# Two linear attentions: transposes in another bank, VectorE's work reordered, GpSimd's rotated sum split

## The chip, the cores and the metric

The kernel runs on one core of a Trainium2 chip. The metric is the device time of one execution in microseconds; the kernel before has a median of 1056.55 us over three runs. All data is float32.

## The reference

`x` has 16 batches of 512 tokens of 128 features. Two blocks follow one another, each an attention and a feed-forward part, both around layer norms, shifts and scales that depend on the batch. The change touches the two attentions alone:

```python
def _linear_attention(q, k, v):
    def step(carry, qkv_t):
        S, z = carry
        qt, kt, vt = qkv_t
        S = S + kt[..., :, None] * vt[..., None, :]
        z = z + kt
        num = jnp.einsum('bhi,bhij->bhj', qt, S)
        den = jnp.sum(qt * z, axis=-1, keepdims=True)
        return ((S, z), num / (den + EPS))
...
q = jax.nn.elu(to_tbhd(q)) + 1.0
k = jax.nn.elu(to_tbhd(k)) + 1.0
...
q = _rotate(q, cos, sin)
k = _rotate(k, cos, sin)
retention = jnp.einsum('bhsd,bhtd->bhst', q, k) * SCALING
retention = retention * decay[None]
out = jnp.einsum('bhst,bhtd->bhsd', retention, v)
out = (out - mean) * jax.lax.rsqrt(var + EPS)
gate = jax.nn.silu(x @ Wg.T)
return gate * out @ Wo.T
```

The first is a causal linear attention with 16 heads of 8 features and the feature map elu + 1. The second is a causal retention with rotated queries and keys, a group norm per head and a gate. `_rotate(x)` is x times a cosine plus the half-swapped x times a sine: two products and a sum.

## The kernel before

A function `attention` (line 291) writes both, with `layer` 0 and 1. A batch is four tiles of 128 tokens, a pair is two tiles, and a step works on one pair `(b, u)`, with tiles `ta = 2u` and `tb = 2u + 1`. I call u = 0 step A and u = 1 step B. Each engine has its own program in order (`pe_step`, `act_step`, `vec_step`, `pool_step`, lines 672 to 790); the engines meet by semaphores alone. A loop runs over the middle batches, and the first and last ones are written out.

For one tile: TensorE projects q, k and v of the next batch's tile into the bank pQ (`pe_qkv`, 410). ScalarE copies v out (`act_qkv`, 419). In the first attention it makes exp and relu of q and k there, and VectorE joins them to the feature map (`vec_qk`, 446). In the second VectorE makes three products with cosines and sines into `ra` and `rb` (452, 456, 457), and GpSimd adds them for q and k of both tiles of a pair (`pool_rope`, 465). pQ is one bank: the next projection waits until it has been read (`qk_free`).

GpSimd then makes all outer products of k and v for a pair (`pool_kv`, 475). TensorE sums them along tokens with a triangular matrix, three matrix products per tile, which I call the states (`pe_states`, 485), into the banks pS. VectorE multiplies each by q (`vec_product`, 574), GpSimd adds the halves of the result (`pool_halve`, 591) and VectorE reduces them (`vec_sum`, 602).

What earlier tiles contribute goes through a running state: `pe_state_sum` (500) adds the tile's key times value in pR, VectorE masks it (`vec_state`, 583), and `pe_inter` (493) multiplies it with the transposed queries into the bank pI, from where ScalarE copies it (`act_inter`, 538). The queries are transposed by `pe_transpose_q` (512) into the fourth quarter of pQ and copied out as qT by `act_qT` (546). Since TensorE must not write into a bank that is being read, this transpose waits until the next batch's tile has left pQ (`v_ready`, `qk_free`).

Two steps later the normalised y is transposed in pairs into pI (`pe_transpose_y`, 521) and copied out (`act_yT`, 553 or 556); in the second attention GpSimd multiplies it by the gate at the end of its step (`pool_gate`, 564). Three steps later it is projected (`pe_project`, 530) and added to x (`vec_residual`, 653). The gate is a silu over a whole batch, once per batch at the end of ScalarE's step A, between two loads of its function tables (`act_gate`, 665 and 666); step B begins behind it.

The order of one step of VectorE is: products 0, 1 and 2 of tile ta, with the feature map or rotation of the pair ahead's second tile behind the first or second of them, then reductions, mask, products of tile tb, and behind its second product the feature map or rotation of the next batch's tile ta.

## Time and profile before

| what | us |
|---|---|
| median of three runs (1055.17 to 1057.34) | 1056.55 |
| profiled execution | 1054.64 |
| its span | 1052.8 |
| PE busy | 860.5 (82%) |
| DVE busy | 829.7 (79%) |
| POOL busy | 711.0 (68%) |
| ACT busy | 609.6 (58%) |

PE is TensorE, DVE VectorE, ACT ScalarE, POOL GpSimd, PEld TensorE's weight loads. Products of the first attention's tiles run from 53.6 us on, and the last of the second attention's start at 675.5; between the two lies the first feed-forward part. "Idle before" in brackets is how long the engine stood still in front of an instruction, and behind the arrow what ended it. Instructions of one engine may overlap by some hundredths of a microsecond, so the distance of two starts is the better price of a step. An "x6" merges instructions of one line, and some matrix products are missing from the trace.

### The profile page before, as it was taken

Reading aid. Unit: us, or ns where it says so; the run is one execution under the profiler, and the core shown is the slowest. Engines: PE = TensorE matmul, PEld = TensorE weight load, DVE = VectorE, ACT = ScalarE, POOL = GpSimd, SP = SyncE. Lnnn points to the kernel's source line nnn. Section 1 sums busy time; section 2 is a strip of 40 time slices with the busy share of each in tenths; the row PEclk is TensorE's granted clock in tenths of the full one; section 3 lists DMA queues with packets and bytes.
Section 4 is the critical chain, followed back from the end, with each engine's and each line's share of the span. In section 5 each row is a group of like instructions: output and inputs, shape, how many; then the busy total and the mean of one; then the engine's idle time right before and its main releaser. Section 6 shows DMA issues by size and latency. Waiting matters only on the chain. (4 is left out here: it accounts for less than half of the span.)

```text
span 1052.8 us, 24355 instructions
## 1 busy us (share of the span) xinstructions
PE 860.5 (82%) x5240; PEld 622.6 (59%) x5240; DVE 829.7 (79%) x2581; ACT 609.6 (58%) x1524; POOL 711.0 (68%) x450
## 2 busy tenths in 40 slices
PE   5699999999968977888898988639888731999993
PEld 5456666666645754555555655426656521999993
DVE  5468888888875994888888888767988770899995
ACT  2545555555427965565656566347765212999992
POOL 4478878878853535999999999645599562255554
PEclk9799999999987998999999999859999855999997
DMA  8520000000000000000000000064566654544420
GB/s 243 165 66 2 0 0 0 0 0 0 0 1 5 0 1 1 11 11 20 10 20 10 20 10 20 21 184 109 149 207 208 192 193 143 159 131 134 133 68 20
DMA packets 64934, 70.11 MB, mean 67 GB/s; under 512 B 8965, under 2 KB 52178, under 8 KB 64740
## 3 DMA queue, kind: packets, MB, share of 16 engines
q1 hardware_dynamic: 50612, 47.20, 16.2%
q0 software_dynamic: 6368, 16.89, 4.7%
q10 hardware_dynamic: 7872, 5.08, 1.7%
q8 instruction: 33, 0.54, 0.2%
q14 instruction: 49, 0.40, 0.1%
HBM read 32.32 MB, written 24.50 MB: 54 GB/s over the span
## 5 line engine op out<-in xcount | busy, mean ns | idle before, releaser
L475 POOL TENSOR_TENSOR a_kv<-a_qk,a_vv 128x2304 f32<-128x2304 f32 (+1 forms) x64 | 252.0, 3938 | 37.1 <-DVE a_qk L446 32.6
L485 PE MATMUL a_pS<-a_kv,utri 128*128 128x360 f32 (+3 forms) x768 | 259.7, 475 | 10.7 <-POOL a_kv L475 10.7
L574 DVE TENSOR_TENSOR a_tt<-a_pS,a_qk 128x360 f32<-128x360 f32 (+3 forms) x384 | 201.5, 527 | 75.4 <-PE a_pS L485 75.2
L485 PEld LDWEIGHTS a_pS<-a_kv,utri 128*128 128x128 f32 x768 | 140.5, 191 | 96.2 <-issue 29.8
L591 POOL TENSOR_TENSOR a_tt<-a_tt 128x1152 f32<-128x1152 f32 (+1 forms) x64 | 144.7, 2260 | 37.7 <-DVE a_tt L574 37.6
L2016 POOL DMA_INDIRECT out_dram<-x_o,x_place x71 | 69.1, 974 | 76.1 <-DVE x_o L2003 75.1
L602 DVE TENSOR_REDUCE a_nd<-a_tt 128x144 f32<-128x720 f32 (+3 forms) x128 | 104.3, 817 | 1.0 <-POOL a_tt L591 0.9
L538 ACT ACTIVATE a_tt<-a_pI 128x144 f32<-128x144 f32 (+1 forms) x96 | 39.8, 415 | 96.0 <-PE a_pI L493 95.9
L1596 POOL DMA_INDIRECT ys<-m_S,m_dest x64 | 63.0, 984 | 35.2 <-issue 12.7
L546 ACT ACTIVATE a_qT<-a_pQ 128x128 f32<-128x128 f32 x96 | 26.5, 276 | 98.9 <-PE a_pQ L410 83.3
L1954 PE MATMUL x_pZ<-w,x_hT 128*128 x568 | 75.9, 277 | 1.4 <-issue 1.4
L1905 ACT ACTIVATE x_w<-w 128x644 f32 x71 | 52.4, 740 | 31.4 <-PEq L1737 26.3
L1954 PEld LDWEIGHTS x_pZ<-w,x_hT 128*128 128x128 f32 x568 | 69.0, 192 | 1.9 <-issue 1.7
L410 PE MATMUL a_pQ<-W,a_hT 128*128 128x384 f32 x122 | 55.2, 535 | 12.6 <-issue 7.2
L410 PE MATMUL a_pQ<-wqkv,a_hT 128*128 128x384 f32 x122 | 55.5, 537 | 8.5 <-issue 4.5
L380 ACT ACTIVATE a_xn<-X,nmr,rstd 128x128 f32 (+1 forms) x128 | 60.8, 484 | 1.8 <-DVE nmr L275 1.8
L287 DVE BATCH_NORM_STATS2 bn<-X 128x6 f32<-128x128 f32 (+1 forms) x256 | 55.9, 273 | 4.8 <-DMA X<-xs 4.7
L465 POOL TENSOR_TENSOR a_qk<-a_ra,a_rb 128x512 f32<-128x512 f32 x32 | 40.7, 1270 | 26.6 <-DVE a_rb L457 16.8
L530 PEld LDWEIGHTS a_pO<-wgate,a_yT 128*128 128x128 f32 x256 | 39.8, 199 | 26.3 <-issue 12.4
L530 PE MATMUL a_pO<-wgate,a_yT 128*128 (+1 forms) x256 | 41.4, 286 | 13.6 <-DVE a_y L644 11.7
L1936 ACT ACTIVATE x_hT<-x_pA,x_w 128x128 f32<-128x128 f32 x142 | 43.8, 360 | 8.4 <-PE x_pB L1928 8.2
L1945 DVE TENSOR_SCALAR x_hT<-x_pB,x_w 128x128 f32<-128x128 f32 x142 | 42.8, 343 | 6.8 <-PE x_pB L1928 6.8
(299 smaller groups left out, 2103.4 us busy)
## 6 DMA issues: line engine op xcount, KB each, us to landing
x_yl<-ys SPq DMA_DIRECT2D x71, 193.5 KB, 2.4
X<-xs SPq DMA_DIRECT2D x16, 256.0 KB, 5.3
kx<-m_kc SPq DMA_DIRECT2D x64, 64.0 KB
ax<-m_pc SPq DMA_DIRECT2D x64, 64.0 KB
m_S<-X SPq DMA_DIRECT2D x16, 256.0 KB, 3.6
xs<-X SPq DMA_DIRECT2D x15, 256.0 KB
w<-in_L_ffn_W_dram SPq DMA_DIRECT2D x1, 2048.0 KB
m_S<-gw ACTq DMA_DIRECT2D x6, 256.0 KB, 2.9
```

What stands on the lines that cost most here:

```text
L287: v.bn_stats(K.bn[:, ds(n, 1), :].rearrange("p a f -> p (a f)"), x[:, ds(n, 1), :].rearrange("p a f -> p (a f)"))\
L380: act.activation(xn[:, t, :], tile(K.X, 4 * b + t), ACT.Identity, bias=column(K.nmr, 4 * b + t), scale=column(K.rstd, 4 * b + t)).then_inc ...
L410: pe.matmul(bank_of(b, t, start)[:, 0:3 * P], hT[:, t * P:(t + 1) * P], wqkv, start=True, stop=True).then_inc(qkv_ps, 1)
L475: pool.tensor_tensor(kv[:, t:t + 2, :, :, :].rearrange("p t h j i -> p (t h) j i"), kk.unsqueeze(2).to_broadcast([P, 2 * H, J, D]), rows.u ...
L485: pe.matmul(pS[c][:, 0:(h1 - h0) * SC], K.utri[:, :], flat[:, h0 * SC:h1 * SC], start=True, stop=True).then_inc(u_done, 1)
L530: mm = pe.matmul(pO[:, k * P:(k + 1) * P], yT[:, k, :], tile(K.wgate[:, 0 if layer == 0 else 2, :, :], b), start=True, stop=True)
L574: v.tensor_tensor(tt[:, t, h0:h1, :, 0:D], pS[c][:, 0:(h1 - h0) * SC].rearrange("p (h j i) -> p h j i", i=D, j=J), q[:, h0:h1, :].unsqueez ...
L591: pool.tensor_tensor(two(D // 2), two(D // 2), two(0), ALU.add).then_inc(half_done, 1)
L602: v.tensor_reduce(nd[:, t % 2, :, :], tt[:, t, :, :, D // 2:rows], AX.X, ALU.add).then_inc(red_done, 1)
L1596: pool.indirect_dma_start(out=A["ys"], out_offset=bass.IndirectOffsetOnAxis(ap=dest[:, g // 2 % 2, at:at + 1], axis=0), in_=S[:, 4 * (g % ...
L1954: mm = pe.matmul(pZ[j % 2][:, 0:P], hT[:, j % 2, c * P:(c + 1) * P], K.w2[:, ds(e, 1), c, :].rearrange("p a f -> p (a f)"), start=(c == 0) ...
L2016: pool.indirect_dma_start(out=token_rows, out_offset=bass.IndirectOffsetOnAxis(ap=place[:, j:j + 1], axis=0), in_=o[:, j % 4, :], in_offse ...
```

## The change

1. The query transpose writes to pI, behind the inter-tile product, and no longer to pQ. It waits for pI's readers in place of pQ's. The projection loses its wait for `qT_ready`.
2. TensorE projects the next batch's tile directly behind the state sum. The output projection, the gate, the transposes of y and the query transpose follow. In the first attention the two tiles of y are transposed in the two halves of the step and copied out one by one; in the second both in the second half.
3. VectorE makes the feature map or rotation of the next batch's tile ta before the products of tile tb; the residual moves behind the mask.
4. In the second attention VectorE adds the rotated products of the queries (`vec_rope_q`), GpSimd those of the keys. A semaphore `q_ready` tells of the queries.
5. ScalarE copies v before qT, and takes the normalisation and the copies of y to the end of a half; the silu with its table loads stands behind both.
6. GpSimd multiplies by the gate one step later, at the step's beginning, before the keys' sum.

```diff
@@ waits of pe_qkv, vec_qk
-                wait(pe, qT_ready, 3 * b - 3 + t)
+                wait(v, q_ready, 2 * b + t // 2)
@@
+        def vec_rope_q(v, b, u):
+            t = 2 * u
+            v.wait_ge(rope_read, 4 * b + t + 2)
+            v.wait_ge(rope_b, 2 * (4 * b + t + 2))
+            wait(v, t_done, 3 * (4 * b + t - 2))
+            wait(v, q_T, 3 * b - 3 + t + 1)
+            v.tensor_tensor(qk[:, 0, t:t + 2, :], ra[:, :, 0:P], rb[:, :, 0:P], ALU.add).then_inc(q_ready, 1)
@@ pool_rope
-            slot_free(pool, b, t + 1)
-            four = lambda r: r[:, :, :].rearrange("p t (a f) -> p a t f", a=2)
-            pool.tensor_tensor(qk[:, :, t:t + 2, :], four(ra), four(rb), ALU.add).then_inc(qk_ready, 1)
+            wait(pool, kv_ready, 2 * b - 2 + u + 1)
+            wait(pool, p_done, 3 * b - 3 + min(t + 2, 3))
+            pool.tensor_tensor(qk[:, 1, t:t + 2, :], ra[:, :, P:2 * P], rb[:, :, P:2 * P], ALU.add).then_inc(qk_ready, 1)
@@ pe_transpose_q
-            pe.wait_ge(v_ready, m)
-            pe.wait_ge(qk_ready, qk_count(b, t))
-            pe.wait_ge(qk_free, m)
+            pe.wait_ge(q_ready, qk_count(b, t))
+            wait(pe, inter_ready, 3 * b + t - 1)
             wait(pe, qT_ready, 3 * b + t - 1)
-            pe.transpose(pQ[:, QT:QT + P], qk[:, 0, t, :], K.ident[:, :]).then_inc(q_T, 1)
+            wait(pe, yT_read, y_issued(b, t - 1))
+            pe.transpose(pI[:, QT:QT + P], qk[:, 0, t, :], K.ident[:, :]).then_inc(q_T, 1)
@@ pe_transpose_y
+            evacuated(pe, b, t)
+            if layer == 0:
+                pe.transpose(pI[:, YT:YT + P], y[:, t % 2, :], K.ident[:, :]).then_inc(y_T, 1)
+            else:
+                pe.transpose(pI[:, YT:YT + P], y[:, 0, :], K.ident[:, :])
+                pe.transpose(pI[:, YT + P:YT + 2 * P], y[:, 1, :], K.ident[:, :]).then_inc(y_T, 1)
@@ vec_step
             if layer == 1 and late:
                 vec_qk(v, *late)
+                vec_rope_q(v, last[0] + 1, last[1])
...
             if cur:
                 vec_state(v, b, ta)
+            if out:
+                vec_residual(v, *out)
             if last:
                 vec_sum(v, last[0], 2 * last[1] + 1)
+            if cur and known(b, 1):
+                vec_qk(v, b + 1, ta)
             if cur:
                 vec_product(v, b, tb, 0)
...
                 vec_product(v, b, tb, 1)
-                if known(b, 1):
-                    vec_qk(v, b + 1, ta)
@@ pool_step
+            if layer == 1 and out:
+                pool_gate(pool, *out, (phase + (u - 3) // 2) % 3)
             if ahead:
                 if layer == 1:
                     pool_rope(pool, *ahead)
                 pool_kv(pool, *ahead)
-            if layer == 1 and back:
-                pool_gate(pool, *back, (phase - 1) % 3)
```

Here `evacuated` waits for the inter-tile copy, for qT and for the copies of y, and `y_issued` counts the transposes of y that come before a tile. The following lists show how the instructions now stand; a row is line, operation and output<-inputs.

TensorE in the first attention, step B of the second batch, first tile up to the next states: a_pS are the states, a_pO the output projection, a_pR the state sum, a_pQ and a_pI the banks. Before:

```order
L485 MATMUL a_pS<-a_kv,utri 128x432
L485 MATMUL a_pS<-a_kv,utri 128x360 x2
L530 MATMUL a_pO<-wgate,a_yT 128x128 x2
L493 MATMUL a_pI<-a_R,a_qT 128x144
L500 MATMUL a_pR<-a_vv,a_qk 128x144
L512 MATMUL a_pQ<-ident,a_qk 128x128
L410 MATMUL a_pQ<-wqkv,a_hT 128x384
L521 MATMUL a_pI<-ident,a_y 128x128 x2
```

The same place on TensorE now:

```order
L494 MATMUL a_pS<-a_kv,utri 128x432
L494 MATMUL a_pS<-a_kv,utri 128x360 x2
L506 MATMUL a_pI<-a_R,a_qT 128x144
L514 MATMUL a_pR<-a_vv,a_qk 128x144
L410 MATMUL a_pQ<-wqkv,a_hT 128x384
L547 MATMUL a_pO<-wgate,a_yT 128x128 x2
L536 MATMUL a_pI<-ident,a_y 128x128
L523 MATMUL a_pI<-ident,a_qk 128x128
```

The projection of q, k and v has moved from behind the query transpose to directly behind the state sum, and the query transpose to the end, into pI.

VectorE in the second attention, step B of the second batch, from the first reduction (a_nd) to the reduction of the variances (a_vs); a_ra and a_rb are the rotations of the next batch's tile, a_tt the products. Before:

```order
L602 TENSOR_REDUCE a_nd<-a_tt 128x128
L574 TENSOR_TENSOR a_tt<-a_pS,a_qk 128x48x8
L574 TENSOR_TENSOR a_tt<-a_pS,a_qk 128x40x8
L452 TENSOR_TENSOR a_ra<-a_pQ,rope_c 128x256
L456 TENSOR_TENSOR a_rb<-a_pQ,rope_s 128x32x4
L457 TENSOR_TENSOR a_rb<-a_pQ,rope_s 128x32x4
L627 TENSOR_REDUCE a_vs<-a_sq 128x32
```

The same step of VectorE now, from its first product on:

```order
L591 TENSOR_TENSOR a_tt<-a_pS,a_qk 128x48x8
L453 TENSOR_TENSOR a_ra<-a_pQ,rope_c 128x256
L457 TENSOR_TENSOR a_rb<-a_pQ,rope_s 128x32x4
L458 TENSOR_TENSOR a_rb<-a_pQ,rope_s 128x32x4
L466 TENSOR_TENSOR a_qk<-a_ra,a_rb 128x256
L591 TENSOR_TENSOR a_tt<-a_pS,a_qk 128x40x8 x2
L619 TENSOR_REDUCE a_nd<-a_tt 128x128
L600 TENSOR_TENSOR a_R<-a_pR,blk 128x128
L670 TENSOR_TENSOR X<-a_pO,X 128x256
L619 TENSOR_REDUCE a_nd<-a_tt 128x128
L453 TENSOR_TENSOR a_ra<-a_pQ,rope_c 128x256
```

The sum of the rotated queries (466) is new, and the next batch's rotation now begins straight behind the second reduction.

ScalarE in the second attention, end of a step A: a_vv is the copy of v, wgate the silu, a_tt the inter-tile copy that opens step B. Before:

```order
L546 ACTIVATE a_qT<-a_pQ 128x128
L61 REGISTER_ALU
L419 ACTIVATE a_vv<-a_pQ 128x128
L61 REGISTER_ALU
L665 ACT_TABLE_LOAD
L665 ACTIVATE wgate<-a_pT 128x512
L666 ACT_TABLE_LOAD
```

The same place on ScalarE now:

```order
L419 ACTIVATE a_vv<-a_pQ 128x128
L559 REGISTER_ALU
L561 ACTIVATE a_qT<-a_pI 128x128
L61 REGISTER_ALU
L381 ISA
L381 REGISTER_ALU
L381 ACTIVATE a_xn<-X,nmr,rstd 128x128
L572 ACTIVATE a_yaff<-a_pI,cols 128x256
L61 REGISTER_ALU
L682 ACT_TABLE_LOAD
L682 ACTIVATE wgate<-a_pT 128x512
L683 ACT_TABLE_LOAD
```

A normalisation (a_xn) and the scaled copy of y (a_yaff) now stand ahead of the first table load.

## Rows read from the trace of the kernel before

**Rows 1.** Busy us by stretch: PE, PEld, DVE, ACT, POOL; then PEclk, DMA share, GB/s.

```profile
100.00:200.00 100.00, 94.84 (x397) 61.07 (x396) 85.09 (x218) 53.63 (x156) 81.25 (x26) 1.00 0.00 0
500.00:600.00 100.00, 88.83 (x382) 58.77 (x383) 86.28 (x228) 61.35 (x142) 90.89 (x49) 1.00 0.05 16
```

**Rows 2.** Timeline of TensorE, first attention: start, us, instruction, idle before.

```profile
203.90 0.30 PE L512 MATMUL a_pQ<-ident,a_qk 128*128 128x128 f32 x1 [0.35 <-DVE a_qk L446]
204.95 2.10 PE L485 MATMUL a_pS<-a_kv,utri 128*128 128x432 f32 x6
206.89 0.61 PE L530 MATMUL a_pO<-wgate,a_yT 128*128 x4
207.33 0.41 PE L493 MATMUL a_pI<-a_R,a_qT 128*128 128x144 f32 x2
207.82 0.27 PE L512 MATMUL a_pQ<-ident,a_qk 128*128 128x128 f32 x1
208.01 0.91 PE L410 MATMUL a_pQ<-wqkv,a_hT 128*128 128x384 f32 x2
208.97 2.10 PE L485 MATMUL a_pS<-a_kv,utri 128*128 128x432 f32 x6
211.69 0.88 PE L410 MATMUL a_pQ<-wqkv,a_hT 128*128 128x384 f32 x2 [0.37 <-issue]
212.41 0.60 PE L388 MATMUL a_pT<-ident,a_xn 128*128 128x128 f32 x4
```

**Rows 3.** The same timeline, VectorE.

```profile
205.88 0.61 DVE L574 TENSOR_TENSOR a_tt<-a_pS,a_qk 128x432 f32<-128x432 f32 x1 [0.70 <-PE a_pS L485]
207.04 0.42 DVE L446 SCALAR_TENSOR_TENSOR a_qk<-a_pQ,a_eb 128x256 f32<-128x256 f32 x1
211.18 0.41 DVE L446 SCALAR_TENSOR_TENSOR a_qk<-a_pQ,a_eb 128x256 f32<-128x256 f32 x1
213.91 0.61 DVE L574 TENSOR_TENSOR a_tt<-a_pS,a_qk 128x432 f32<-128x432 f32 x1 [1.15 <-PE a_pS L485]
```

**Rows 4.** Timeline of VectorE, second attention, step A.

```profile
527.25 0.56 DVE L574 TENSOR_TENSOR a_tt<-a_pS,a_qk 128x384 f32<-128x384 f32 x1 [0.61 <-PE a_pS L485]
531.91 1.03 DVE L574 TENSOR_TENSOR a_tt<-a_pS,a_qk 128x384 f32<-128x384 f32 x2 [0.43 <-PE a_pS L485]
535.66 0.56 DVE L574 TENSOR_TENSOR a_tt<-a_pS,a_qk 128x384 f32<-128x384 f32 x1 [0.36 <-PE a_pS L485]
```

**Rows 5.** The same stretch, ScalarE and TensorE around the silu.

```profile
520.36 1.28 ACT L666 ACT_TABLE_LOAD   x1
522.20 0.41 PE L521 MATMUL a_pI<-ident,a_y 128*128 128x128 f32 x2 [0.78 <-ACT a_tt L538]
525.15 0.88 PE L410 MATMUL a_pQ<-W,a_hT 128*128 128x384 f32 x2 [0.60 <-issue]
535.02 0.28 ACT L546 ACTIVATE a_qT<-a_pQ 128x128 f32<-128x128 f32 x1 [0.67 <-PE a_pQ L410]
535.48 1.28 ACT L665 ACT_TABLE_LOAD   x1
537.39 1.28 ACT L666 ACT_TABLE_LOAD   x1
```

**Rows 6.** Groups by line: ScalarE's normalisation and scaling of yT.

```profile
L380 ACT ACTIVATE a_xn<-X,nmr,rstd 128x128 f32 (+1 forms) x128 | 60.8, 484 | 1.8 <-DVE nmr L275 1.8
L556 ACT ACTIVATE a_yaff<-a_pI,cols 128x256 f32<-128x256 f32 x32 | 18.0, 563 | 5.5 <-PE a_pI L521 5.4
```

**Rows 7.** Timeline of GpSimd, second attention: the product with the gate.

```profile
534.03 0.72 POOL L564 TENSOR_TENSOR a_yT<-a_yaff,wgate 128x256 f32<-128x256 f32 x1
```

**Rows 8.** Token shift: line 987 (ns min/median/max), then the timeline of one meeting.

```profile
L987 DVE SCALAR_TENSOR_TENSOR f_xr<-f_d,cols,f_h x16: 744/747/1102, 325.5 to 383.6; 128x512 f32<-128x512 f32 x16
...
383.50 0.62 POOL L1016 TENSOR_TENSOR f_ka<-f_kr 128x256 f32<-128x256 f32 x1 [0.64 <-ACT f_kr L1005]
383.56 1.10 DVE L987 SCALAR_TENSOR_TENSOR f_xr<-f_d,cols,f_h 128x512 f32<-128x512 f32 x1
```

More of the change, by code:

```diff
@@ L491, in pe_inter @@
             pe.wait_ge(r_ready, 3 * b + t)
-            wait(pe, yT_read, 2 * b + t // 2 - (1 if t % 2 else 2))
+            wait(pe, yT_read, y_issued(b, t))
             pe.matmul(pI[:, 0:H * J], qT[:, :], R[:, :, :].rearrange("p h j -> p (h j)"),
@@ L642, in vec_y @@
             v.wait_ge(rec_done, n + 1)
-            wait(v, y_T, n)
+            wait(v, y_T, 2 * n if layer == 0 else n)
             v.tensor_tensor(y[:, :, :].rearrange("p t (h j) -> p (t h) j", h=H),
@@ L674, in pe_step @@
             cur, back, out = pair(b, u, 0), pair(b, u, -2), pair(b, u, -3)
-            if cur and not first:
-                pe_states(pe, b, ta)
-            if out:
-                pe_project(pe, *out)
             if cur:
+                if not first:
+                    pe_states(pe, b, ta)
                 if ta > 0:
@@ L682, in pe_step @@
                 pe_state_sum(pe, b, ta)
-                pe_transpose_q(pe, b, ta + 1)
                 if known(b, 1):
                     pe_qkv(pe, b + 1, ta)
-            if back:
-                pe_transpose_y(pe, back, b, u)
+            if out:
+                pe_project(pe, *out)
+            if cur and layer == 1 and u == 0 and known(b, 1):
+                pe_gate(pe, b + 1)
+            if back and layer == 0:
+                pe_transpose_y(pe, back, b, ta)
             if cur:
-                if layer == 1 and u == 0 and known(b, 1):
-                    pe_gate(pe, b + 1)
+                pe_transpose_q(pe, b, ta + 1)
                 pe_states(pe, b, tb)
@@ L699, in pe_step @@
                     pe_transpose_x(pe, b + 2)
+            if back:
+                pe_transpose_y(pe, back, b, tb)
+            if cur and tb < 3:
+                pe_transpose_q(pe, b, tb + 1)
         def act_step(act, b, u, phase, more=True):
@@ L708, in act_step @@
                     act_inter(act, b, ta)
-                if more:
-                    act_normalise(act, b + 2, ta)
-                act_qT(act, b, ta + 1)
                 if known(b, 1):
                     act_qkv(act, b + 1, ta)
-            if back:
-                act_yT(act, *back)
+                act_qT(act, b, ta + 1)
+            if back and layer == 0:
+                act_yT(act, *back, 0)
+            if more:
+                act_normalise(act, b + 2, ta)
             if layer == 1 and last:
@@ L719, in act_step @@
                 act_inter(act, b, tb)
-                if more:
-                    act_normalise(act, b + 2, tb)
             if layer == 1 and last:
@@ L724, in act_step @@
             if cur:
+                if known(b, 1):
+                    act_qkv(act, b + 1, tb)
                 if tb < 3:
                     act_qT(act, b, tb + 1)
-                if known(b, 1):
-                    act_qkv(act, b + 1, tb)
-                if layer == 1 and u == 0 and known(b, 1):
-                    act_gate(act, b + 1, (phase + 1) % 3)
+            if more:
+                act_normalise(act, b + 2, tb)
+            if back:
+                act_yT(act, *back, 1)
+            if cur and layer == 1 and u == 0 and known(b, 1):
+                act_gate(act, b + 1, (phase + 1) % 3)
         def vec_step(v, b, u):
@@ L745, in vec_step @@
                 vec_qk(v, *late)
-            if out:
-                vec_residual(v, *out)
             if cur:
@@ L761, in vec_step @@
                 vec_product(v, b, tb, 1)
-                if known(b, 1):
-                    vec_qk(v, b + 1, ta)
+            if layer == 0 and done:
+                vec_stats(v, *done, 1)
             if last:
@@ L768, in vec_step @@
                     vec_var(v, *last)
-            if layer == 0 and done:
-                vec_stats(v, *done, 1)
             if cur:
@@ L780, in pool_step @@
         def pool_step(pool, b, u, phase):
-            last, back, ahead = pair(b, u, -1), pair(b, u, -2), pair(b, u, 1)
+            last, out, ahead = pair(b, u, -1), pair(b, u, -3), pair(b, u, 1)
             if last:
                 pool_halve(pool, *last)
+            if layer == 1 and out:
+                pool_gate(pool, *out, (phase + (u - 3) // 2) % 3)
             if ahead:
@@ L849, in _ @@
                     vec_qk(v, 0, t, start=True)
+                    if layer == 1 and t % 2:
+                        vec_rope_q(v, 0, t // 2)
                 for b in range(2):
@@ L885, in _ @@
                             pool_step(pool, 3 * i + 2 + k, 1, 2 + k)
-                for b in range(B - 2, B + 1):
+                for b in range(B - 2, B + 2):
                     for u in range(2):
```

40 lines of the change are left out of this document (20 added, 20 removed).

## The prediction, written before the changed kernel had run

> **What bounds the kernel now.** I first read the busy times by stretch [rows 1]. In the loop of the first attention TensorE is busy 94.84 of 100 us at full clock, VectorE 85.09, GpSimd 81.25. In the second attention it is 88.83, 86.28 and 90.89: three engines near their limit, so what counts is how they wait for each other. I then read the timelines of one batch in each loop. A batch is two pairs of token tiles, called step A (tiles 0, 1) and step B (tiles 2, 3).
>
> In the first attention one cycle explains the period. VectorE's first product of a step begins at 205.88, the next at 213.91 after 1.15 us of idleness [rows 3]: 8.03 us per step. Between them VectorE works through to the feature map of the next batch's tile at 211.18, which ends near 211.6; the next qkv projection begins at 211.69 after a wait, x transposes follow at 212.41, and 1.50 us later VectorE gets its first product [rows 2, 3]. In the other step the query transpose stands in front of the projection and waits 0.35 us for that same feature map [rows 2], because both use the bank pQ. So VectorE's late feature map holds back TensorE, and then VectorE waits for TensorE.
>
> In the second attention a batch takes 17.03 us, from one second table load (520.36) to the next (537.39) [rows 5]. Step A takes 8.41 us, with marked waits of 0.43 and 0.36 [rows 4]. Step B begins under a silu between two table loads; TensorE's transposes of y wait 0.78 us for the inter-tile copy behind them, and a projection later 0.60 us for VectorE's rotation [rows 5].
>
> **The first attention, part by part.** The query transpose leaves pQ, and VectorE makes the next batch's feature map before the products of the second tile instead of after two of them. That takes the cycle above apart; what remains is TensorE's own pace. From [rows 2]: states 1.94 (204.95 to 206.89), output projection 0.44, inter-tile product and state sum 0.49 together (half of it each), query transpose 0.19, qkv with two y transposes 0.96, qkv alone 0.72, so 0.12 for a y transpose.
>
> One new wait appears. The projection now stands right behind the state sum, and needs the other feature map, which stays behind two products: its end is 1.58 us after VectorE's first product [rows 3], that begins 0.93 after the states (204.95 to 205.88), and 0.10 passes until TensorE starts (211.59 to 211.69 [rows 2, 3]). That is 2.61 us after the states begin. In step A TensorE would be there at 1.94 + 0.25 = 2.19 and waits 0.42; in step B at 2.43 and waits 0.18. Step A: 2.61 + 0.72 + 0.44 + 0.12 + 0.19 = 4.08, then 1.94 + 0.49 + 0.72 + 0.12 + 0.19 = 3.46, together 7.54. Step B: 4.08 + 1.94 + 0.25 + 0.72 = 6.99, then 1.50 + 0.12 from the x transposes to VectorE's product, less the 0.93 with which I count from product to product: 7.68. A batch takes 15.22 against 16.06 (twice 8.03), **0.84 less**. VectorE's 85.09% of 16.06 is 13.7 us, GpSimd's less: both fit. Splitting the y transposes adds no work; the extra ScalarE instruction stands on an engine that is busy 53.63 of 100 us [rows 1]. Queued behind the transposes' new waits for the inter-tile copy are the next states; TensorE's qkv, 0.72 us, covers that copy, and without that cover the states would slip by the copy. Were the new waits of 0.42 and 0.18 not there, the gain would be 1.44; were the old cycle merely replaced by another as long, 0.
>
> **The second attention, part by part.** GpSimd's rotated sum is halved. GpSimd's product with a gate, 128x256, takes 0.72 [rows 7]; the key sum has that shape, so I take 0.7. It takes GpSimd off the edge and I count it as nothing more, since the moved gate product now stands before it. VectorE gets a new 128x256 sum; an instruction of that shape takes 0.42 there [rows 3]. Step A for VectorE alone: 8.41 - 0.43 - 0.36 + 0.42 = 8.04, so a batch is at least 16.08, a gain of 0.95.
>
> ScalarE gives some of it back. The first table load starts 8.23 after the step's first product (527.25 to 535.48). The 0.67 of waiting in front of qT at 535.02 [rows 5] goes, since the projection comes earlier. But a normalisation of 0.48 and the scaling of yT of 0.56 [rows 6] now stand ahead of the load: it starts at 8.60. Load, silu and load take 3.19 (535.48 to the end of 537.39), and 0.56 pass to TensorE's start (521.64 to 522.20): 12.35. What waits there is now the query transpose, and behind it the second tile's states. From there to the next first product it is 5.05 now (522.20 to 527.25), less the 0.60 that the rotation cost: 16.80, a gain of 0.23. The ends are 0.23 and 0.95; neighbouring ScalarE instructions overlap somewhat in the rows, so I take **0.55**, near the middle.
>
> **The shared port.** The new sum reads two SBUF tensors, and no VectorE instruction in the loops of the attentions does now. The token shift shows what that means: a VectorE instruction with two SBUF inputs takes 0.75 (median), and once 1.10, when GpSimd's f_ka had started 0.06 us before it and ran 0.62 [rows 8]. It ended 0.54 after GpSimd's. So such a sum waits for a GpSimd instruction that is under way. The Trainium skill, page "SBUF — State Buffer", section "Who interferes with whom", states this as a rule: a VectorE instruction with two SBUF inputs contends with a GpSimd instruction that reads SBUF, and whichever issues second blocks for the whole of the other. The trace agrees (1.10 against 0.75). In the new order the sum follows the last rotation on its own engine, while GpSimd's key sum must hear of that rotation from another engine: VectorE should be first there. It may meet the end of the halving or the gate product. I count up to 0.1 per step for it, inside the 0.55.
>
> **Sum.** Of 16 batches the first and the last lack a neighbour, so I count 14: 14 x 0.84 = 11.8, 14 x 0.55 = 7.7, together 19.5. The profiled execution took 1054.64 (its span is 1052.8, and the 1.84 around it stay), which gives 1035.1; the median of the runs shown is 1056.55, 1.9 above it, which gives **1037.0**.
>
> **Rivals.**
> *The second attention gains nothing.* ScalarE's chain above gives back the 0.95, or each sum waits for one gate product of 0.72: 2 x (8.04 + 0.72) = 17.52 per batch, 0.49 more than now. The total is then 1056.55 - 11.8 = 1045 to 1056.55 - 11.8 + 6.9 = 1052. For it speaks that the gate product now stands directly before the key sum; against it that in step B VectorE has room while ScalarE holds TensorE.
> *Slower: the port holds VectorE in every pair.* If GpSimd, never idle between instructions, keeps the port through gate product and key sum, VectorE's sum waits 0.72 + 0.7 per pair: 2 x (8.04 + 1.42) = 18.92, 1.89 more per batch, so + 26.5 - 11.8: 1071.2. It decides from a mean wait of 0.9 per pair on, where 14 x (2 x (8.04 + 0.9) - 17.03) = 11.9 eats the first attention's gain. The one instance [rows 8] proves waiting, not that GpSimd keeps the port from one instruction to the next. The Trainium skill's rule above, applied to a sum that always issues second, would give this same time.
> *No change.* The change may not do what it says: in both attentions VectorE's work stays as long, and the projection of the first tile waits as long as the transpose did. 1056.5. Against it: 1.15 us of VectorE's idleness per step [rows 3] has no other cause.
>
> **How the numbers follow.** Forecast, both attentions gain: 0.52, from 1028 (the first attention at 1.44, the second at 0.55: 14 x 1.99 = 28) to 1045. Only the first gains: 0.25, 1045 to 1052. No change: 0.09. Port: 0.14. About 0.2% is what a measurement of this kernel can tell from no change. Faster by more is 0.52 + 0.25 = 0.77, within it 0.09, slower 0.14. Together the likely cases and the nearer half of no change reach from 1028 to 1055, with under 2 in 10 left out. The forecast's own range is 1028 to 1045.
>
> **What would show it.** Right: in the first attention, states follow each other at 15.2 to 15.5 us per batch, the query transpose never waits for VectorE's feature map, and the projection behind the state sum waits 0.2 to 0.4. In the second, 16.1 to 16.8 per batch, VectorE's new sum at 0.42 to 0.5, the query transpose of step B waiting over 1 us for the inter-tile copy after the silu. Wrong: new sums of VectorE of 1 us and more, or idleness of VectorE in front of its products as large as before.

## The result and the profile after

The change makes the kernel slower. Four runs of the changed kernel have a median of 1083.14 us (1082.63 to 1083.54), four of the kernel before beside them 1056.3: a ratio of 1.0254, 95% interval 1.0236 to 1.0272. Forecast were 1037.0, with 1028 to 1055 as the range. In one run below, the one with the sum behind the product, one of six times (2906.81 us) stands far apart; it is in that run's median and not in its ratio.

Where the time went is read from two starts that frame the stages: the first and last normalisation of the first feed-forward part (f_xn) and the first of the next (m_xn), from the view of one tile's instructions. Its lines end with the first and last start, first of the kernel before, then of the changed one:

```profile
L959 ACT ACTIVATE f_xn<-X,nmr,rstd x64: 480/485/495, 319.6 to 379.2; 128x128 f32 x40, 128x128 f32<-128x128 f32 x24
L1316 ACT ACTIVATE m_xn<-X,nmr,rstd x64: 477/480/494, 696.4 to 802.0; 128x128 f32<-128x128 f32 x64
```

```profile
L984 ACT ACTIVATE f_xn<-X,nmr,rstd x64: 480/486/495, 334.7 to 394.3; 128x128 f32 x40, 128x128 f32<-128x128 f32 x24
L1341 ACT ACTIVATE m_xn<-X,nmr,rstd x64: 477/481/497, 724.7 to 831.5; 128x128 f32<-128x128 f32 x64
```

| us | first attention ends (first f_xn) | first to last f_xn | second attention (last f_xn to first m_xn) |
|---|---|---|---|
| before | 319.6 | 59.6 | 317.2 |
| after | 334.7 | 59.6 | 330.4 |

The first attention lost 15.1 us where 11.8 of gain were forecast, the second 13.2 where 7.7 were. The busy times by stretch, in the columns of [rows 1], show every engine slacker in the first attention; in the second VectorE alone is a little fuller (86.97 against 86.28):

```profile
100.00:200.00 100.00, 87.99 (x363) 56.12 (x362) 80.57 (x204) 50.72 (x155) 75.04 (x24) 1.00 0.00 0
500.00:600.00 100.00, 85.36 (x360) 54.60 (x358) 86.97 (x229) 61.30 (x138) 82.60 (x45) 1.00 0.05 13
```

TensorE fell from 94.84 to 87.99. So something new is waited for. TensorE's timeline in the first attention, at the end of step B and the start of the next step A (the place of 211.69 to 212.41 in [rows 2]):

```profile
203.53 0.49 PE L389 MATMUL a_pT<-ident,a_xn 128*128 128x128 f32 x3
205.16 0.33 PE L389 MATMUL a_pT<-ident,a_xn 128*128 128x128 f32 x1 [1.15 <-ACT a_xn L381]
205.37 0.30 PE L536 MATMUL a_pI<-ident,a_y 128*128 128x128 f32 x1
205.98 2.20 PE L494 MATMUL a_pS<-a_kv,utri 128*128 128x432 f32 x6 [0.31 <-issue]
208.01 0.41 PE L514 MATMUL a_pR<-a_vv,a_qk 128*128 128x144 f32 x2
208.81 0.88 PE L410 MATMUL a_pQ<-wqkv,a_hT 128*128 128x384 f32 x2 [0.39 <-DVE a_qk L446]
```

Three of the four x transposes run, and the fourth stands still for 1.15 us until ScalarE has normalised the fourth tile. Then the states start another 0.31 late, with no engine named. ScalarE's timeline at the same place shows what stood before that normalisation:

```profile
203.73 0.28 ACT L419 ACTIVATE a_vv<-a_pQ 128x128 f32<-128x128 f32 x1 [0.21 <-PE a_pQ L410]
203.90 0.38 ACT L424 ACTIVATE a_ea<-a_pQ 128x256 f32<-128x256 f32 x1
204.31 0.42 ACT L427 ACTIVATE a_eb<-a_ea 128x256 f32<-128x256 f32 x1
204.63 0.48 ACT L381 ACTIVATE a_xn<-X,nmr,rstd 128x128 f32 x1
```

The change has put the normalisation of tile tb behind these three, which wait for the projection. TensorE has its x transposes directly behind that same projection. In the kernel before, the same normalisation started ahead of the projection (211.69 in [rows 2]) and was done when the x transposes came:

```profile
211.58 0.49 ACT L380 ACTIVATE a_xn<-X,nmr,rstd 128x128 f32 x1
```

VectorE in the changed kernel, the columns as in [rows 3]:

```profile
205.78 0.42 DVE L661 TENSOR_TENSOR a_y<-a_nd,a_pO 128x256 f32<-128x256 f32 x1 [1.46 <-PE a_pI L536]
207.09 0.61 DVE L591 TENSOR_TENSOR a_tt<-a_pS,a_qk 128x432 f32<-128x432 f32 x1 [0.89 <-PE a_pS L494]
214.84 0.61 DVE L591 TENSOR_TENSOR a_tt<-a_pS,a_qk 128x432 f32<-128x432 f32 x1 [0.47 <-PE a_pS L494]
```

VectorE pays twice. Its new y waits 1.46 for the transpose of the old one, which queues behind the x transposes, and its next product waits 0.89. Step A takes 7.75 (207.09 to 214.84; forecast 7.54). GpSimd's outer products of one batch start at 199.35, of the next at 216.59: 17.24 per batch, so step B takes 9.49 (forecast 7.68).

In the second attention the same transpose waits:

```profile
526.73 0.33 PE L389 MATMUL a_pT<-ident,a_xn 128*128 128x128 f32 x1 [0.56 <-ACT a_xn L381]
```

VectorE's timeline of the step that follows, and the start of the next (the place of [rows 4]), with its new sum at line 466:

```profile
528.59 0.56 DVE L591 TENSOR_TENSOR a_tt<-a_pS,a_qk 128x384 f32<-128x384 f32 x1 [0.71 <-PE a_pS L494]
...
530.16 0.97 DVE L466 TENSOR_TENSOR a_qk<-a_ra,a_rb 128x256 f32<-128x256 f32 x1 [0.28 <-DVE a_rb L458]
...
537.06 0.55 DVE L591 TENSOR_TENSOR a_tt<-a_pS,a_qk 128x384 f32<-128x384 f32 x1
...
538.67 0.73 DVE L466 TENSOR_TENSOR a_qk<-a_ra,a_rb 128x256 f32<-128x256 f32 x1 [0.34 <-DVE a_rb L458]
```

GpSimd beside it, the gate (580) and the keys' sum (474):

```profile
530.13 0.72 POOL L474 TENSOR_TENSOR a_qk<-a_ra,a_rb 128x256 f32<-128x256 f32 x1 [1.18 <-DVE a_rb L458]
...
538.39 0.73 POOL L580 TENSOR_TENSOR a_yT<-a_yaff,wgate 128x256 f32<-128x256 f32 x1
539.08 0.92 POOL L474 TENSOR_TENSOR a_qk<-a_ra,a_rb 128x256 f32<-128x256 f32 x1
```

Both of VectorE's sums end 0.28 after GpSimd's instruction that was under way: 531.13 against 530.85, and 539.40 against 539.12. In step B GpSimd's own sum then takes 0.92, since VectorE's was under way when it started. The groups by line, shapes apart:

```profile
L474 POOL TENSOR_TENSOR a_qk<-a_ra,a_rb 128x256 f32<-128x256 f32 x32 | 27.7, 865 | 25.0 <-DVE a_rb L458 25.0
L466 DVE TENSOR_TENSOR a_qk<-a_ra,a_rb 128x256 f32<-128x256 f32 x32 | 24.8, 775 | 8.2 <-DVE a_rb L458 8.0
```

VectorE's sum takes 0.775 in the mean where I put 0.42, and waits 0.25 in the mean for its own last rotation, which I had left out. It was not held every time: of the thirteen steps A from 458 to 675 us, VectorE's sum came 0.03 ahead of GpSimd's in four (at 512.39, for one). It then took 0.42 or 0.43, and GpSimd's sum took 0.98.

### The profile page after: what moved, and what is told of

Same layout as the page of the kernel before. It is cut to its first block and busy times, and to the rows that moved or that the text cites. A ratio compares the mean times of both kernels' runs of the same rounds, so it can differ in the third digit from the quotient of the medians.

```text
span 1080.8 us, 24873 instructions
## 1 busy us (share of the span) xinstructions
PE 865.8 (80%) x5240; PEld 622.0 (58%) x5240; DVE 851.7 (79%) x2613; ACT 618.0 (57%) x1556; POOL 698.5 (65%) x450
## 5 line engine op out<-in xcount | busy, mean ns | idle before, releaser
L494 PE MATMUL a_pS<-a_kv,utri 128*128 128x360 f32 (+3 forms) x768 | 262.8, 479 | 15.7 <-POOL a_kv L484 9.9
L591 DVE TENSOR_TENSOR a_tt<-a_pS,a_qk 128x360 f32<-128x360 f32 (+3 forms) x384 | 196.5, 525 | 39.4 <-PE a_pS L494 36.4
L494 PEld LDWEIGHTS a_pS<-a_kv,utri 128*128 128x128 f32 x768 | 136.4, 191 | 93.2 <-issue 35.8
L419 ACT ACTIVATE a_vv<-a_pQ 128x128 f32<-128x128 f32 x122 | 33.9, 278 | 100.4 <-PE a_pQ L410 100.4
L1930 ACT ACTIVATE x_w<-w 128x644 f32 x71 | 52.4, 740 | 31.4 <-PEq L1762 26.4
L410 PE MATMUL a_pQ<-wqkv,a_hT 128*128 128x384 f32 x122 | 52.4, 512 | 9.0 <-DVE a_qk L446 5.6
L389 PE MATMUL a_pT<-ident,a_xn 128*128 128x128 f32 x128 | 27.4, 298 | 35.0 <-ACT a_xn L381 35.0
L661 DVE TENSOR_TENSOR a_y<-a_nd,a_pO 128x256 f32<-128x256 f32 x64 | 26.8, 418 | 30.5 <-PE a_pI L536 19.0
```

The source lines that it names most:

```text
L410: pe.matmul(bank_of(b, t, start)[:, 0:3 * P], hT[:, t * P:(t + 1) * P], wqkv, start=True, stop=True).then_inc(qkv_ps, 1)
L494: pe.matmul(pS[c][:, 0:(h1 - h0) * SC], K.utri[:, :], flat[:, h0 * SC:h1 * SC], start=True, stop=True).then_inc(u_done, 1)
L591: v.tensor_tensor(tt[:, t, h0:h1, :, 0:D], pS[c][:, 0:(h1 - h0) * SC].rearrange("p (h j i) -> p h j i", i=D, j=J), q[:, h0:h1, :].unsqueez ...
```

## The experiments

Two theories stood after that reading. N: the late normalisation costs nearly all, through the fourth x transpose, and with it TensorE's loop turn (its way from the end of the loop's body back to the start) comes into the open. P: VectorE's new sum, held up by GpSimd, costs a smaller part, in the second attention alone. All runs were compared with the kernel before on the same chip. The stages, in the columns of the table above:

| run | median (before) | ratio, interval | first attention ends | f_xn | second attention |
|---|---|---|---|---|---|
| normalisation early | 1048.01 (1054.29) | 0.9943, 0.9923 to 0.9963 | 316.8 | 57.2 | 317.3 |
| before, normalisation late | 1107.46 (1054.29) | 1.0493, 1.0463 to 1.0523 | 349.6 | 57.6 | 342.4 |
| one sum | 1078.32 (1054.29) | 1.0205, 1.0164 to 1.0245 | 335.8 | 57.2 | 326.6 |
| early, one sum | 1038.48 (1054.29) | 0.985, 0.9821 to 0.988 | 316.0 | 57.8 | 307.5 |
| the same on another chip | 1040.72 (1054.39) | 0.989, 0.9862 to 0.9917 | 315.6 | 57.1 | 308.7 |
| early, sum behind product | 1044.44 (1056.2) | 0.9886, 0.9854 to 0.9918 | 315.1 | 56.9 | 310.5 |
| early, VectorE first | 1043.44 (1056.2) | 0.9874, 0.985 to 0.9898 | 315.2 | 57.0 | 310.9 |
| early, one sum, x last | 1048.12 (1056.2) | 0.9908, 0.9876 to 0.994 | 316.5 | 59.6 | 309.6 |
| early, one sum, turn by three | 1035.12 (1054.39) | 0.9832, 0.98 to 0.9863 | 311.7 | 57.0 | 305.9 |
| early, behind and first | 1039.03 (1054.39) | 0.9862, 0.9833 to 0.989 | 316.0 | 57.1 | 307.4 |
| the change with all three | 1034.75 (1056.06) | 0.9804, 0.9786 to 0.9821 | 311.9 | 59.7 | 306.5 |
| before, turn by three | 1052.25 (1056.06) | 0.9973, 0.9956 to 0.9991 | 318.3 | 57.0 | 317.3 |

**The normalisation back to its place.** The change, with one line moved:

```diff
                 act_inter(act, b, tb)
+            if more:
+                act_normalise(act, b + 2, tb)
...
-            if more:
-                act_normalise(act, b + 2, tb)
             if back:
                 act_yT(act, *back, 1)
```

> The changed kernel with ScalarE's normalisation of the second tile put back to where it stood before, right behind the inter-tile copy and ahead of the copies of v (both attentions). Theory N (in step B TensorE's last x transpose waits for that normalisation, which the change put behind the projection's copies; 1.27 us of standing still and about 0.3 us of loop turn behind it in the first attention, 0.8 and 0.3 in the second): 14 x 1.6 + 14 x 1.0 = 36 us less than the change, about 1047; a batch of the first attention falls from 17.2 to about 15.6 us. Theory P (the port: VectorE's new sum waits for GpSimd and that is the loss): the first attention, which has no such sum, stays at 17.2 us and the total within 5 us of 1083.

This line alone is worth 17.9 us in the first attention (334.7 to 316.8) and 13.1 in the second (330.4 to 317.3), and takes the change from 1.0254 to 0.9943 of the kernel before. Against that kernel the first attention is now 2.8 us shorter and the second the same; another 2.4 lie in the feed-forward part, which the change does not touch. N holds.

**The same line in the kernel before.** Its normalisation of tb moved behind the projection's copies, nothing else:

```diff
                 act_inter(act, b, tb)
-                if more:
-                    act_normalise(act, b + 2, tb)
...
                 if known(b, 1):
                     act_qkv(act, b + 1, tb)
+                if more:
+                    act_normalise(act, b + 2, tb)
```

> The kernel before with this one move of the change alone: the second tile's normalisation goes behind the copies of v (and of the feature map). Theory N: TensorE's last x transpose of a batch waits about 1.4 us in the first attention and 0.6 to 0.9 in the second, plus the loop turn that is no longer hidden: 14 x 1.6 + 14 x 1.0 = about 33 to 36 us more than before, about 1090. If VectorE's late feature map covers a part of it, at least 10 us more. Theory P: no change, 1056.

It costs 53 us, more than I expected. TensorE's timeline at the end of a step B of the first attention, and then its busy times from 232 us on, in the columns of [rows 1]:

```profile
232.01 0.33 PE L388 MATMUL a_pT<-ident,a_xn 128*128 128x128 f32 x1 [1.15 <-ACT a_xn L380]
232.63 3.89 PE L485 MATMUL a_pS<-a_kv,utri 128*128 128x432 f32 x6 [0.28 <-issue]
```

```profile
232.00:237.00 5.00, 4.70 (x13) 2.77 (x14) 1.72 (x4) 1.16 (x2) 1.33 (x2) 0.66 0.00 0
```

The wait is the same 1.15, and the turn of 0.28 behind it too. From the batch before (the same transpose at 214.24) it is 17.77. In the kernel before, a batch takes 16.00, from 212.41 in [rows 2] to this row:

```profile
228.41 0.60 PE L388 MATMUL a_pT<-ident,a_xn 128*128 128x128 f32 x4
```

That gives 14 x 1.77 = 24.8 us. In four of the fourteen batches, the states behind this gap then take 3.8 to 3.9 in place of 2.20, at a mean granted clock of 0.66 in this stretch, that is, partly at 1.2 GHz. These four batches are 1.6 to 1.7 longer than the others, 6.6 together. The two give 31.4; the first attention is 30.0 longer. The clock falls here in states that follow the 1.15 of standing still; in the changed kernel, with the same wait, it stays at 1.00 in the two stretches shown above. Why it falls in four batches and not in the others is not shown.

The second attention is 25.2 longer. The fourth transpose waits only 0.42 to 0.48 there, but a batch takes 18.63 against 17.05; through what the rest of this comes was not followed.

**One sum on GpSimd.** The changed kernel with the rotated sum of queries and keys in one instruction of GpSimd, as before:

```diff
-        q_ready = qk_ready if layer == 0 else sem("q_ready")
+        q_ready = qk_ready
...
-                vec_rope_q(v, last[0] + 1, last[1])
...
-            pool.tensor_tensor(qk[:, 1, t:t + 2, :], ra[:, :, P:2 * P], rb[:, :, P:2 * P], ALU.add).then_inc(qk_ready, 1)
+            pool.tensor_tensor(qk[:, :, t:t + 2, :], four(ra), four(rb), ALU.add).then_inc(qk_ready, 1)
```

> The changed kernel with the rotated sums again made by GpSimd alone for queries and keys (one 128x512 instruction), everything else as changed. Theory P: the second attention's loss (18.24 us per batch against 17.03) goes, about 1066 or less. Theory N: the sum's price in VectorE (0.73 in the median instead of the 0.42 expected, plus about 0.3 of waiting for its own rotation) is worth at most 0.5 to 1.0 per pair where VectorE bounds, and step B is bound elsewhere: 1070 to 1085.

Undoing the split gains 3.8 us in the second attention while the late normalisation is still there. With the normalisation early it gains more, so the late normalisation hid a part of it:

> Both edits: the normalisation put back and GpSimd making the whole rotated sum. Theory N with the port as the smaller second term: the first attention as in the run with the normalisation alone (about 15.6 per batch), the second about 0.5 us per batch faster than there, so about 1040. If the new split was worth having once the x transposes no longer wait, this run is slower than the one with the normalisation alone. Theory P: equal to the run with the one sum.

The second attention goes from 317.3 to 307.5, by 9.8 us. So the rest of the change gains 9.7 there (317.2 to 307.5), and the split, meant as help, spends it. Run again on another chip, this version had 308.7:

> The version with the early normalisation and one sum on GpSimd once more, as the base for the two runs beside it on the same chip: 0.985 of the kernel before if chips do not differ in this, near 0.988 if the chip of the other three runs was what cost 2 us.

**What the split pays for: two ways around it.** First, VectorE's sum behind its next product:

```diff
                 vec_qk(v, *late)
-                vec_rope_q(v, last[0] + 1, last[1])
             if cur:
                 vec_product(v, b, ta, 1)
+            if layer == 1 and late:
+                vec_rope_q(v, last[0] + 1, last[1])
```

> The version with the early normalisation (1048.0, second attention 317.3 us), with VectorE's sum of the queries moved behind its next product, so that it follows no rotation of its own. Theory S (the sum's cost is its wait of 0.28 to 0.34 for its own engine's last rotation, plus 0.42): the wait is gone at 26 places, the sum stays where it was in length, about 8 us less, 1040. Theory P (the sum costs what GpSimd holds it up): in step A it now begins near 505.3 by that version's times, with GpSimd's key sum over at 505.5 and the product of keys and values (3.71 us) starting at 505.6; where the sum meets that product it takes 3 us and more, and the second attention gets slower: with half of the sums caught, 14 x 3 = 42 us more, 1090. If the maximum of line 466 stays under 1.5 us and the time falls by 8, S is right and P explains only the length.

Second, GpSimd's sum made to wait for VectorE's:

```diff
             wait(pool, p_done, 3 * b - 3 + min(t + 2, 3))
+            pool.wait_ge(q_ready, 2 * b + u + 1)
             pool.tensor_tensor(qk[:, 1, t:t + 2, :], ...
```

> The version with the early normalisation (1048.0), with one wait more: GpSimd's key sum waits for VectorE's query sum, so that VectorE goes first. Theory P (an instruction of VectorE with two SBUF inputs is held by a GpSimd instruction under way): in step A the sum falls from 0.98 to 0.42, since the key sum was what held it; in step B the gate product is still under way at the sum's start, so 0.72 stays. GpSimd's key sum and its product of keys and values come about 0.45 later; where they have slack, 14 x 0.55 = 7.7 us less, 1040; where states wait for them, no gain, 1048 or some us more. Rival (the sum is slow by itself with two SBUF inputs of 256 elements a row): 0.98 and 0.72 stay as they are.

The first gains 6.8 us, the second 6.4. The groups by line, first of the sum behind the product, then of VectorE first:

```profile
L466 DVE TENSOR_TENSOR a_qk<-a_ra,a_rb 128x256 f32<-128x256 f32 x32 | 24.4, 762 | 0.1
```

```profile
L466 DVE TENSOR_TENSOR a_qk<-a_ra,a_rb 128x256 f32<-128x256 f32 x32 | 20.7, 648 | 8.3 <-DVE a_rb L458 8.0
```

Behind the product, the wait of 8.0 us for the own rotation is gone and the length is not. Theory S (the sum waits for its own engine's last rotation) holds for the wait, and P for the length. The collision with the product of keys and values that P feared did not come; the longest sums were 0.94, apart from one at the start. With VectorE first, the sums of 0.97 are gone from the loop (the last of all still takes that long): of 22 from 451 to 625 us half took 0.42 or 0.43, the other half, which meet the gate, still 0.72 to 0.74. The rival, that such a sum is slow by itself, falls. Both together:

> The version with the early normalisation and VectorE's sum both behind its next product and ahead of GpSimd's key sum. If the two gains (6.8 and 6.4 us of the second attention, each against 317.3) are of different costs, the wait of 0.28 to 0.34 and the hold by the key sum, they add up: second attention near 304, in all 1036, and the split would then equal the version with one sum. If they are two ways out of the same cost, the second attention stays near 310 and the time near 1043; GpSimd's key sum then comes 0.5 later and its products hold the next states.

```profile
L466 DVE TENSOR_TENSOR a_qk<-a_ra,a_rb 128x256 f32<-128x256 f32 x32 | 15.5, 483 | 0.1
```

Now all 22 take 0.41 to 0.43, the prediction's price, and the wait is gone. But the second attention stands at 307.4, not near 304: no better than one sum on GpSimd (308.7 on this chip). GpSimd's sum now waits longer for VectorE's, 32.2 us in all against 24.4 with VectorE first alone; that this is what holds the stage was not tried. So the two gains add up in part, and a split without its costs is worth 1.3 us, about what the stage with one sum differs from run to run (307.5 and 308.7).

**The loop turn.** With the normalisation early, TensorE still stands still between the last transpose of step B and the next states. Early normalisation and one sum, first attention:

```profile
208.28 0.64 PE L389 MATMUL a_pT<-ident,a_xn 128*128 128x128 f32 x4
208.80 0.30 PE L536 MATMUL a_pI<-ident,a_y 128*128 128x128 f32 x1
209.40 2.20 PE L494 MATMUL a_pS<-a_kv,utri 128*128 128x432 f32 x6 [0.30 <-DVE a_tt L591]
```

0.60 lie between the two starts, where the query transpose and the states of step B have 0.2. In the kernel before there is no such gap: the states follow 0.48 after the first of four x transposes (212.41 in [rows 2]):

```profile
212.89 2.20 PE L485 MATMUL a_pS<-a_kv,utri 128*128 128x432 f32 x6
```

I first took it for too short a queue and moved the x transposes behind the transpose of y:

```diff
-                if u == 1 and known(b, 2):
-                    pe_transpose_x(pe, b + 2)
             if back:
                 pe_transpose_y(pe, back, b, tb)
+            if cur and u == 1 and known(b, 2):
+                pe_transpose_x(pe, b + 2)
```

> The version with the early normalisation and one sum on GpSimd (1038.5), with TensorE's four transposes of x moved from before to behind the transpose of y that ends step B. Theory L (TensorE's loop turn is uncovered in step B, because its queue has nothing left but that one transpose, and the wait of 0.31 marked issue in front of the next states is that turn): the wait goes down to 0.1 or less, the first attention gets about 0.3 per batch shorter, 4 us, 1034; the chain of scaled y of ScalarE gets 0.5 earlier too. Rival (the loop's end is set by VectorE's products, and TensorE's turn is only where the waiting shows): no difference over 1 us, and the wait is then marked with VectorE.

That failed: the first attention is 0.5 longer than on the first chip, not 4 shorter. TensorE there:

```profile
208.80 0.66 PE L389 MATMUL a_pT<-ident,a_xn 128*128 128x128 f32 x4
209.74 2.20 PE L494 MATMUL a_pS<-a_kv,utri 128*128 128x432 f32 x6 [0.28 <-issue]
```

The four transposes start 0.12 apart and the gap remains. Is it the turn at all? Three batches to a turn decides it:

```diff
-                with pe.Fori(2, B - 2) as b:
-                    pe_step(pe, b, 0)
-                    pe_step(pe, b, 1)
+                with pe.Fori(0, (B - 4) // 3) as i:
+                    for k in range(3):
+                        pe_step(pe, 3 * i + 2 + k, 0)
+                        pe_step(pe, 3 * i + 2 + k, 1)
```

> The version with the early normalisation and one sum on GpSimd, with TensorE's loop written with three batches in a turn where there was one (as ScalarE's and GpSimd's loops are in the second attention). Theory L2 (the 0.46 between the last transpose of step B and the next states is TensorE's loop turn, which is uncovered because no long instruction stands behind the last wait): of 12 batches 8 lose the gap of about 0.4 in each attention, 2 x 8 x 0.4 = 6.4 us less than that version run on the same chip; in the trace two of three batches have the states within 0.15 of the last transpose, and the third keeps 0.4. Rival (the states wait there for a product of VectorE, as the trace of that version marks it in the first attention): the gap is the same in all batches, and the time within 2 us.

```profile
205.87 0.65 PE L389 MATMUL a_pT<-ident,a_xn 128*128 128x128 f32 x4
206.39 0.30 PE L536 MATMUL a_pI<-ident,a_y 128*128 128x128 f32 x1
206.61 2.20 PE L494 MATMUL a_pS<-a_kv,utri 128*128 128x432 f32 x6
...
221.31 0.65 PE L389 MATMUL a_pT<-ident,a_xn 128*128 128x128 f32 x4
221.83 0.30 PE L536 MATMUL a_pI<-ident,a_y 128*128 128x128 f32 x1
222.46 2.20 PE L494 MATMUL a_pS<-a_kv,utri 128*128 128x432 f32 x6 [0.33 <-DVE a_tt L591]
```

Inside a turn the states follow after 0.22, at its edge after 0.63, in the trace in every third batch. The "DVE" in the bracket is the nearest semaphore, not the cause: the same wait is absent inside a turn. The time falls from 1040.72 to 1035.12, by 5.6 where 6.4 were expected (3.9 in the first attention, 2.8 in the second). So the wait is the loop's turn, as theory L2 says, and a batch inside a turn takes 15.44 (205.87 to 221.31, from x transposes to x transposes): close to the forecast's 15.22. The control is the same edit in the kernel before:

> The kernel before with TensorE's loop three batches to a turn and nothing else. If the loop turn costs only where no long instruction stands behind the last wait (theory L2), it is free here: the projection of 0.72 stands between the last wait and the transposes of x, and the states follow 0.44 to 0.49 after the first transpose, without a gap; time within 0.2% of before. If the turn costs in any loop, 2 x 8 x 0.4 = 6 us less, ratio 0.994.

The ratio of 0.9973 is lower than expected, but not by the loop. In the profiled execution the feed-forward part, which the edit doesn't touch, is 2.6 shorter, more than the whole span's 2.4. The second attention is the same within 0.1. The first is 1.3 shorter, and has this lead already at its first x transposes (38.30 against 39.62), before the loop begins. In the loop a batch takes 16.07 (98.39 to 226.94 are eight), no less than the 16.00 of before, and the states follow 0.43 to 0.51 after the x transposes' start, where it was 0.48. So the turn is covered there. That the cover is the long projection between the last wait and the turn fits this and the failed try; it was not tried by itself.

**All three out of the change.** Normalisation early, the sum behind and first, three batches to a turn:

> The change with its three costs taken out: normalisation early, VectorE's sum behind its next product and ahead of GpSimd's key sum, TensorE's loop three batches to a turn. If the turn's 6 us (8 gaps in each attention) add to the version without it (1039.0 where the kernel before took 1054.4): 1033, ratio 0.980; states behind step B's last transpose within 0.25 in two of three batches. If the split sum takes the place of the turn as the bound in the second attention, only the first attention gains, 4 us: 1035.

It takes 1034.75, the lowest ratio of the study, and the second of the two cases expected came: three batches to a turn gain 4.1 in the first attention (316.0 to 311.9) and 0.9 in the second (307.4 to 306.5). Here the split stays, on equal terms with one sum (0.9832, interval 0.98 to 0.9863). Busy times by stretch:

```profile
100.00:200.00 100.00, 95.74 (x404) 62.49 (x404) 89.43 (x225) 54.23 (x175) 83.79 (x27) 1.00 0.00 0
500.00:600.00 100.00, 92.81 (x403) 62.19 (x402) 93.13 (x253) 63.35 (x148) 89.33 (x50) 1.00 0.05 16
```

## Why the prediction was wrong

**The step that failed: "1.50 + 0.12 from the x transposes to VectorE's product".** I moved the x transposes with the rest of step B as if their data lay ready, and costed ScalarE's moved normalisation only where it delays the silu. In the kernel before, it was finished a projection earlier; now it stands behind the projection's copies. In the changed kernel the way from the x transposes to VectorE's product takes 3.56 (203.53 to 207.09) where the sum has 1.62. What stands in it is 1.15 of waiting per batch in the first attention, and 0.4 to 0.8 in the second. That this is the cost is shown by taking it out (31.0 us less over both attentions) and by putting it into the kernel before (53 more). It was no rival of mine at all: the rival that ends slower has the right sign and the wrong cause.

**The loop turn** was the second thing left out. It cost 6.7 us over both attentions for 8 of 12 batches, so by the same price 10 for all. In the first attention the two omissions, 17.9 and 3.9 x 12/8 = 5.9, make 23.8 of the 26.9 by which that stage missed its forecast. The rest is 0.22 per batch inside a turn (15.44 against 15.22), 3.1 us. VectorE's first product stands 1.11 behind the states' start (205.98 to 207.09) where I counted 0.93, and the projection 2.83 (205.98 to 208.81) where I counted 2.61; why was not tried. That these parts add up so exactly is luck: the batch before takes 16.00 and not 16.06, since 8.03 is the longer of its two steps, so 14 x 0.06 = 0.8 of the forecast gain was never there.

**VectorE's new sum at 0.42, with up to 0.1 for the port**, was mis-sized: 0.775 and a wait of 0.25, together 0.60 above the price per pair. Over the stage the split costs 9.8 us once the normalisation is early. The sentence "VectorE should be there first" failed in step A of nine of thirteen batches. After the last rotation starts there, GpSimd's sum begins 0.53 later and VectorE's 0.56 (529.60 is that start): VectorE must wait for its own result as long as GpSimd for VectorE's. The rival "the port holds VectorE" described a part of this with its rows, but all of it together is 0.60 per pair, under the 0.9 from which it would have decided, and 0.25 of that is no hold by GpSimd.

**What held.** The new wait of the projection behind the state sum was forecast at 0.42 in step A and measured at 0.39. Step A of the first attention was forecast at 7.54 and took 7.75. The query transpose no longer waits for the feature map there. In the second attention ScalarE's first table load was to start 8.60 behind step A's first product; it starts 8.82 behind, in this row (528.59 is the product):

```profile
537.41 1.28 ACT L682 ACT_TABLE_LOAD   x1
```

The query transpose of step B then waits 10.4 us in 10 times by the view of waits (440 to 620 us), as the forecast's "over 1 us" had it. It starts 12.52 behind step A's first product (528.59 to 541.11; forecast 12.35), so ScalarE's chain was sized rightly up to there. What followed was not:

```profile
541.11 0.30 PE L523 MATMUL a_pI<-ident,a_qk 128*128 128x128 f32 x1 [1.03 <-issue]
```

```profile
546.78 0.56 DVE L591 TENSOR_TENSOR a_tt<-a_pS,a_qk 128x384 f32<-128x384 f32 x1 [0.71 <-PE a_pS L494]
```

From the query transpose to the next first product it is 5.67 where the forecast had 4.45 (5.05 less 0.60), and 5.01 with the normalisation early (515.31 to 520.32 in that run).

With the three costs out, the reordering gains nearly what was forecast in sum and not in its parts: the first attention ends 7.7 us earlier (forecast 11.8) and the second takes 10.7 less (forecast 7.7). That this kernel takes 1034.75, near the predicted 1037.0, is therefore partly luck, and it is not the kernel that was predicted. With the normalisation alone in its old place it is 1048.01.

## What to carry to other kernels

When an engine's instruction is moved later, list all who read its result, and set its new end against each reader's place in its own queue: a normalisation that is off the critical path everywhere can stand ahead of the one transpose that ends the loop. Look at what stands between the last wait of a loop body and its end: a turn that was covered there can appear when the order changes, and several batches to a turn make it rarer (5.6 us here). Before a sum with two SBUF inputs moves from GpSimd to VectorE, look at what GpSimd does at that moment, and at whether the instruction directly before it on VectorE makes its input.

## What the runs showed of the hardware

An engine's own result is not free: VectorE's sum directly behind its last rotation, for which the program makes it wait by a semaphore, stood still for 0.28 to 0.34, and one product between them took the whole wait away.

The time for which VectorE is held lies inside its instruction, not in front of it. The clearest meeting is at the start of the second attention of the changed kernel, on GpSimd and then on VectorE:

```profile
418.58 3.71 POOL L484 TENSOR_TENSOR a_kv<-a_qk,a_vv 128x2048 f32<-128x2048 f32 x1
```

```profile
420.17 2.40 DVE L466 TENSOR_TENSOR a_qk<-a_ra,a_rb 128x256 f32<-128x256 f32 x1
```

The sum started 1.59 into GpSimd's product and ended at 422.57, again 0.28 behind GpSimd's end at 422.29. The Trainium skill, page "SBUF — State Buffer", section "Who interferes with whom", says that a VectorE instruction with two SBUF inputs contends with a GpSimd instruction that reads SBUF, that the port pair they share is "an exclusive lock", and that the order of issue decides who blocks. The trace agrees, with 0.42 alone, 0.72 to 0.97 behind GpSimd's short instructions and 2.40 here. It agrees in the other direction too: where VectorE's sum started first, GpSimd's took 0.92 to 0.98 against 0.72, and ended 0.6 behind VectorE's end.

The same feed-forward code took 56.9 to 59.7 us. The stretch from 318 to 372 us, first of the run with the sum behind the product (56.9), then of the one with the x transposes last (59.6), in the columns of [rows 1]:

```profile
318.00:372.00 54.00, 49.37 (x316) 38.29 (x317) 45.20 (x111) 51.83 (x114) 27.82 (x28) 1.00 0.00 0
```

```profile
318.00:372.00 54.00, 50.37 (x301) 39.97 (x298) 42.16 (x103) 48.18 (x106) 26.68 (x28) 0.88 0.00 0
```

The granted clock is 1.00 in the one and 0.88 in the other. Over this part of each run's own trace, from first to last f_xn, it is 0.97 or 0.98 in the eight that took 56.9 to 57.2, and 0.88 to 0.91 in the four that took 59.6 or 59.7; the kernel before is one of these four, with 0.91. Differences of 2 or 3 us between these versions can come from there, which is why the stages are compared and not the totals alone.
